# Segment sums of a graph network by pairs of 500 edges and 128 nodes, instead of by steps of 128-edge tiles

## The reference

```python
def _L1_gnn_ref(x, src, dst, ...):            # once
    m = jax.nn.relu(x[src])
    agg = jax.ops.segment_sum(m, dst, num_segments=N)
    h = (1.0 + eps[0]) * x + agg
...
def _L2_gnn_ref(node_feat, ...):              # 4 times
    trans = jnp.einsum('nd,tod->tno', h, W_edge) + b_edge[:, None, :]
    msg = trans[etypes, src]
    a = jax.ops.segment_sum(msg, dst, num_segments=N)
    h = _gru_cell(a, h, W_ih, W_hh, b_ih, b_hh)
```

## Time and profile before

| | |
|---|---|
| median of 3 runs | 12611.91 us |
| lowest and highest of them | 12582.9 and 12612.57 us |
| span of the profiled execution | 12521.9 us |
| outside the span, to the median and to the lowest run | 90.0 and 61.0 us |
| share of the span: PE, DVE, POOL, ACT | 53%, 44%, 50%, 19% |
| clock granted to TensorE, mean | 0.701 |

### The profile page before, as it was taken

The page is one execution under the profiler, slowest core; times in us unless marked ns, Lnnn a source line. Parts: engine busy times, 40 slices in busy tenths (PEclk is TensorE's granted clock), DMA queues, the critical chain, the costliest instruction groups (busy, mean ns, idle before and its releaser), DMA issues. The chain is left out here.

```text
span 12521.9 us, 164892 instructions
## 1 busy us (share of the span) xinstructions
PE 6604.1 (53%) x35059; PEld 5552.8 (44%) x35060; DVE 5536.9 (44%) x13969; ACT 2372.4 (19%) x5039; POOL 6320.5 (50%) x6362
## 2 busy tenths in 40 slices
PE   4555686555686555785335333433533353355555
PEld 3555674555665555663223222333322332234444
DVE  4444664444664444753334233433433343345555
ACT  1222452222452222452000000000000000011111
POOL 2555432556422555423663666366366636635663
PEclk7777898777897777896556555655655565567777
DMA  2333321334322333321111111111111111112221
GB/s 81 113 113 113 99 80 55 116 114 118 101 69 64 114 115 114 102 63 29 44 44 55 46 42 43 56 44 43 47 53 44 43 57 43 43 25 87 82 80 58
DMA packets 697724, 893.26 MB, mean 71 GB/s; under 512 B 148412, under 2 KB 442581, under 8 KB 697500
## 3 DMA queue, kind: packets, MB, share of 16 engines
q0 software_dynamic: 198368, 429.61, 13.4%
q1 hardware_dynamic: 497412, 461.38, 11.8%
q10 hardware_dynamic: 1848, 1.12, 0.0%
HBM read 698.40 MB, written 193.14 MB: 71 GB/s over the span
## 5 line engine op out<-in xcount | busy, mean ns | idle before, releaser
L761 POOL DMA_INDIRECT l_sums_ring<-table_typed,index x2512 | 2436.2, 970 | 1951.2 <-ACT index L862 1181.2
L897 PE MATMUL psum<-l_sums_ring,select 128*128 x6720 | 1630.0, 419 | 3214.3 <-DVE select L793 2600.8
L761 POOL DMA_INDIRECT acc<-table_x,index x2016 | 2039.8, 1012 | 2141.2 <-DVE index L756 1556.4
L897 PEld LDWEIGHTS psum<-l_sums_ring,select 128*128 128x128 f32 x6720 | 1404.0, 309 | 3443.1 <-issue 3443.1
L823 DVE TENSOR_TENSOR acc<-acc,psum 128x128 f32 (+1 forms) x4032 | 1160.8, 288 | 3336.4 <-remote 2288.8
L793 DVE TENSOR_TENSOR select<-iota_row,dst_local 128x512 f32<-128x512 f32 (+1 forms) x1680 | 1070.8, 638 | 340.0 <-issue 318.8
L1015 PE MATMUL psum<-ident,select 128*128 128x128 f32 x2016 | 437.8, 356 | 1465.0 <-DVE acc L974 593.5
L990 DVE TENSOR_TENSOR l_scores_prod<-l_scores_key,psum 128x512 f32<-128x512 f32 x504 | 345.7, 686 | 1777.3 <-ACT l_scores_key L963 1303.7
L862 ACT COPY index<-tile_idx 128x4 int32 (+1 forms) x785 | 150.3, 193 | 4510.2 <-remote 2770.2
L1015 PEld LDWEIGHTS psum<-ident,select 128*128 128x128 f32 x2016 | 300.3, 181 | 1540.3 <-issue 827.3
L761 POOL DMA_INDIRECT l_pass_ring<-table_kv,index x672 | 674.7, 1004 | 598.5 <-issue 242.4
(11 more groups left out here) (319 smaller groups left out, 10103.9 us busy)
## 6 DMA issues: line engine op xcount, KB each, us to landing
acc<-in_edge_attr_dram SPq DMA_DIRECT2D x2016, 64.0 KB
rows_dram<-l_scores_mixT SPq DMA_DIRECT2D x504, 256.0 KB
l_values_ring<-rows_dram SPq DMA_DIRECT2D x504, 256.0 KB
table_typed<-l_rows_rows SPq DMA_DIRECT2D x40, 1024.0 KB, 4.2
l_sums_ring<-table_typed,index POOLq DMA_INDIRECT x2512
acc<-table_x,index POOLq DMA_INDIRECT x2016
l_pass_ring<-table_kv,index POOLq DMA_INDIRECT x672
table_x<-l_rows_rows SPq DMA_DIRECT2D x40, 256.0 KB, 2.2
```

The costliest lines, as they stand in the source:

```text
L761: pool.indirect_dma_start(out=ring[:, at, u, :], out_offset=None, in_=table, in_offset=bass.IndirectOffsetOnAxis(ap=index[:, at % REGIONS, ...
L897: ins = pe.matmul(sums(r, u), select[:, r, u, :], rows, start=True, stop=True)
```

## The change

The edges are cut into 640 tiles of 125 instead of 625 of 128, so that four tiles, a region, are 500 edges and there are exactly 160 regions. The list of the pass is no longer of tiles and blocks but of pairs (region, block): 160 + 40 = 200. For a pair, one select is made over all four tiles of the region against one block, the four products accumulate in one PSUM slice, and one addition goes into `acc`. A region that reaches into a second block is walked again with that block. Register values are read for four pairs at a time.

```diff
-TILE_REGIONS = -(-TILES // GROUP)
+EDGES = 125
+SUM_TILES = E // EDGES
+TILE_REGIONS = SUM_TILES // GROUP
...
-                pool.indirect_dma_start(out=ring[:, at, u, :], out_offset=None, in_=table,
-                                        in_offset=bass.IndirectOffsetOnAxis(ap=index[:, at % REGIONS, u:u + 1], axis=0)
+                pool.indirect_dma_start(out=ring[0:n, at, u, :], out_offset=None, in_=table,
+                                        in_offset=bass.IndirectOffsetOnAxis(ap=index[0:n, at % REGIONS, u:u + 1], axis=0)
...
+                        def pick(s, k, column):
+                            at_least(dve, p_summed, s - (REGIONS - 1))
+                            dve.scalar_tensor_tensor(
+                                out=select[:, k, :, :], in0=dst_all[:, bass.ds(column, GROUP)].unsqueeze(2).broadcast_to([P, GROUP, P]),
+                                scalar=pair_start[:, bass.ds(s, 1)], in1=iota_row[:].unsqueeze(1).broadcast_to([P, GROUP, P]),
+                                op0=ALU.subtract, op1=ALU.is_equal).then_inc(p_selected, 1)
+
+                        def body(i):
+                            last = isinstance(i, int) and i == PAIR_TURNS - 1
+                            entries = by_step(dve, pick_row, (i * REGIONS + 1) * 2, 2 * REGIONS, TILE_REGIONS * GROUP)
+                            for k in range(REGIONS):
+                                s = i * REGIONS + k
+                                to_block, column = entries[2 * k], entries[2 * k + 1]
+                                if not (last and k == REGIONS - 1):
+                                    pick(s + 1, (k + 1) % REGIONS, column.with_bounds(min_val=0, max_val=(TILE_REGIONS - 1) * GROUP))
+                                dve.wait_ge(p_summed, s + 1)
+                                at_least(dve, p_added, s)
+                                to = acc[:, bass.ds(to_block.with_bounds(min_val=0, max_val=BLOCKS) * ACC_W, D)]
+                                dve.tensor_tensor(to, to, sums(k), ALU.add).then_inc(p_added, 1)
-                        make_select(dve, 0, 0)
-
-                        def body(i):
-                            for r in range(REGIONS):
-                                if nxt := led(i, r, 1):
-                                    at_least(dve, p_summed, region_of(*nxt) - (REGIONS - 1))
-                                    make_select(dve, *nxt)
-                                add_blocks(dve, sums, i, r, D, blocks_of(dve, i, r))
-                        turns(dve, body)
...
                     @b.tensor
                     def _(pe):
                         def body(i):
-                            for r in range(REGIONS):
-                                j = region_of(i, r)
-                                needs, *at = by_step(pe, plan_row, j * PLAN, PLAN, TILE_RING * GROUP * D)
-                                pe.wait_ge(p_selected, j + 1)
+                            entries = by_step(pe, sum_row, i * (2 * REGIONS), 2 * REGIONS, TILE_RING * GROUP * D)
+                            for k in range(REGIONS):
+                                s = i * REGIONS + k
+                                needs, at = entries[2 * k], entries[2 * k + 1]
+                                pe.wait_ge(p_selected, s + 1)
                                 pe.wait_ge(p_landed, needs.with_bounds(min_val=1, max_val=TILE_REGIONS))
-                                at_least(pe, p_added, (j - (REGIONS - 1)) * GROUP)
+                                at_least(pe, p_added, s - (REGIONS - 1))
+                                at = at.with_bounds(min_val=0, max_val=(TILE_RING - 1) * GROUP * D)
                                 for u in range(GROUP):
-                                    rows = slots[:, bass.ds(at[u].with_bounds(min_val=0, max_val=(TILE_RING * GROUP - 1) * D), D)]
-                                    ins = pe.matmul(sums(r, u), select[:, r, u, :], rows, start=True, stop=True)
+                                    rows = slots[0:EDGES, bass.ds(at + u * D, D)]
+                                    ins = pe.matmul(sums(k), select[0:EDGES, k, u, :], rows, start=u == 0, stop=u == GROUP - 1)
                                 ins.then_inc(p_summed, 1)
```

More of the change, by code:

```diff
@@ new lines, in _ @@
+                    link(dve.tensor_copy(dst_tf, dst_ti[:]))
+                    dve.sem_inc(s_pair, 1)
+                    dve.wait_ge(s_pair_pe, 1)
+                    for c in range(PAIR_C):
+                        link(dve.tensor_scalar(behind, psum[0:PAIR_K, 4, 0:TILE_REGIONS], pair_no[:, c:c + 1], None, ALU.is_lt))
+                        link(dve.tensor_reduce(pair_at[:, 0, c:c + 1], behind, AX_X, ALU.add))
+                    link(dve.tensor_scalar(pair_at[:, 0, :], pair_at[:, 0, :], float(TILE_REGIONS - 1), None, ALU.min))
@@ L456, in _ @@
                             at = (c % n_bank) * n_row
-                            ins = pe.transpose(psum[:, bank + c // n_bank, at:at + n_row], of[:, c, :], ident[0:n_row, 0:n_row])
+                            wide = P if n_row == ROW_K else EDGES
+                            ins = pe.transpose(psum[0:wide, bank + c // n_bank, at:at + n_row], of[:, c, :], ident[0:n_row, 0:n_row])
                         ins.then_inc(s_pe, 1)
+                    pe.wait_ge(s_pair, 3)
+                    for c in range(TILE_COLS):
+                        at = (c % n_bank) * TILE_ROWS
+                        pe.transpose(psum[0:EDGES, 2 + c // n_bank, at:at + TILE_ROWS], dst_tf[:, c, :], ident[0:TILE_ROWS, 0:TILE_ROWS])
+                    pe.matmul(psum[0:PAIR_K, 4, 0:TILE_REGIONS], ones[0:1, 0:PAIR_K], region_reach[:], start=True, stop=True).then_inc(s_pair_pe, 1)
+                    pe.wait_ge(s_pair, 4)
+                    for c in range(2 * PAIR_C):
+                        ins = pe.transpose(psum[0:1, 5, c * PAIR_K:(c + 1) * PAIR_K], pair_at[:].rearrange("k a c -> k (a c)")[:, c:c + 1],
+                                           ident[0:PAIR_K, 0:PAIR_K])
+                    ins.then_inc(s_pair_pe, 1)
+                    pe.wait_ge(s_pair, 5)
+                    pe.matmul(psum[:, 6, 0:PAIRS], ones[0:1, :], pair_row[:, 1, :], start=True, stop=True).then_inc(s_pair_pe, 1)
         def at_least(eng, sem, value):
@@ L782, in pair @@
                 for k in range(at, at + n):
-                    gather(pool, ring, table, k)
+                    gather(pool, ring, table, k, EDGES)
             with pool.Fori(0, TILE_TURNS) as i:
@@ L910, in gat_score_pass @@
                 key = sb(f"{name}_key", [P, 2, GROUP, D], F32, tmp)
-                prod = sb(f"{name}_prod", [P, GROUP, D], F32, tmp)
+                prod = acc[:, 2 * RING:2 * RING + GROUP * D].rearrange("p (u f) -> p u f", f=D)
                 part = sb(f"{name}_part", [P, GROUP, GAT_HEADS], F32, tmp)
@@ L1044, in gat_value_pass @@
                 msg = sb(f"{name}_msg", [P, REGIONS, GROUP, W], F32, tmp)
-                away = sb(f"{name}_away", [P, 2, GROUP, P], F32, tmp)
+                away = w3[:].rearrange("p (a u) f -> p a u f", a=2)
                 def values(r):
```

139 lines of the change are left out of this document (98 added, 41 removed).

## The result

The changed kernel took 12692.15 us (median of 4 runs, 12674.36 to 12710.38), the kernel before 12612.24 us beside it (4 runs, 12582.9 to 12630.22): a ratio of 1.0067 with a 95% interval of 1.0054 to 1.0079, so 0.67% or 80 us slower. The forecast was 12,770, slower, for reasons that turned out to hold only in part.

A forecast was written before the change was run, and what follows sets the result against it. The prediction took the sum passes as gather streams stopped by PE's late reports; 5 x (15 + 24 - 9) + 10 = +160 us gave a span of about 12,682, plus 90 us, so 12,770, range 12,200 to 13,000.

The forecast's parts named there:

- gathers and gaps between them: First sum pass: 640 gathers of 125 rows at an unchanged 1.25 us instead of 628, +15 us a pass.
- stops: Waits of POOL on a full ring: 35.7 instead of 30 a pass, +24 us, bounds -129 and +54 us.
- rest: Forecast -9 us a pass: credit for DVE's issue gaps, which fall by 83 us while DVE mostly waits for PE.
- the bound of 0.06: Upper bound on POOL's extra time for a gather of 125 rows: +0.06 us a gather, +38 us a pass.
- The sentence by the rule of the Trainium skill: Transfers: 125 rows use 5 DMA engines instead of 16, 0.8 us instead of 0.25, +0.55 us a pass.
- The sign named for this case: In the changed profile: fewer than 27 stops a pass would mean late reports came from DVE or all engines' issue.
- Times five: First-pass terms multiplied over five sum passes: 5 x (15 + 24 - 9) + 10 = +160 us.
- DVE: Sum passes: additions and selects fall from 309 to 196 us a pass, the new select taking 692 ns.
- Table stage: Small DVE operations, PE round trips and loads added once ahead of the passes: +10 us.
- The 90 us outside the span: Median of runs 12611.9 lies 90 us above the span 12521.9, so about 12,682 of span became 12,770.
- DVE is the bound: Rival, sum passes: fewer DVE instructions let pairs keep up with gathers; 12,050, half-way 12,330; chance 0.34, wholly or in part.
- the gather of 125 rows costs POOL more: Rival: +0.06 us on 3200 gathers, +192 us on top of the sum, 12,960; chance 0.05.

## Why the prediction was right in its sign, and where it failed

The first pass by its terms, forecast and measured:

| | before | forecast of the change | measured change |
|---|---|---|---|
| gathers and gaps between them | 805.0 | +15 | 968.6, +163.6 |
| stops | 129.3 | +24 | 0, -129.3 |
| rest | 18.7 | -9 | 7.4, -11.3 |
| pass | 953 | +30 | 976, +23 |

- **Gathers.** The step "if a gather costs POOL the same ... I take 0" failed. It costs 0.24 us more, four times the bound of 0.06 that I took from the rows of 96 and 128. Both counts are multiples of 16, so these rows could not bound the cost of a count that isn't. The sentence by the rule of the Trainium skill said how many engines 125 rows use and stopped at the transfer. From the start of the first region's fourth gather to PE's first product it takes 5861.37 - 5857.63 = 3.74 us, against 2.79 before: +0.95, of which 0.25 are POOL's longer gather, so 0.70 where the estimate by the rule had 0.55. That comes once a pass. What costs the time is POOL's part, 640 times. (The 785 us of the prediction for the gathers of before were measured as 805, so half of its 39 us "for start and tail" were gathers.) These are the rows, changed kernel, then the one before:

```profile
5857.63 1.20 POOL L827 DMA_INDIRECT l_sums_ring<-table_x,index  x1 [0.30 <-issue]
...
5861.37 2.07 PE L983 MATMUL psum<-l_sums_ring,select 125*128 x8 [19.75 <-SPq L919]
```

```profile
5811.54 0.95 POOL L761 DMA_INDIRECT l_sums_ring<-table_x,index  x1 [0.31 <-issue]
...
5814.33 2.07 PE L897 MATMUL psum<-l_sums_ring,select 128*128 x8 [17.53 <-SPq L848]
```

- **Stops.** "What limits them during gathers is PE's lateness, and PE's work a step is the same" was right for gathers of 128 rows: pairs with them had passes of 979 (990 forecast) and 25 stops (35.7 forecast). But the lateness was taken as given, with its cause unnamed, and it went with the row count. The sign named for this case ("if there are fewer than 27 stops a pass, the reports were late because of DVE or of the sum of issues") points to the wrong cause: the steps with 125 rows keep all of DVE's additions and have no stops. The two errors nearly cancel, 163.6 - 129.3 = 34 against 15 + 24 = 39. That the forecast came within 80 us is luck in this sense: a mechanism that it didn't have, the dearer gather, paid for stops that it kept.
- **Times five.** The change was forecast as +160 us and measured as +80. The terms are those of the first pass, which was the shortest of the five before (952.6 us, on average 961) and is not in the changed kernel (976.6, on average 976.4). Its +24 us times five would be 120; the five passes together gave 77.
- **DVE.** Its busy time fell to 199 us a pass (196 forecast). The new select takes 748 ns, not 692. Little of it shows in the pass, as forecast: pairs with 128 rows are not faster than steps with 128 rows (979 against 961, and 0.53% slower in all on one chip).
- **Table stage.** About 4 us instead of 10.
- **The 90 us outside the span.** This reading was wrong. Each run now lists its own time and span, 1.8 us apart (12674.36 and 12672.5). The profiled execution of before, 12521.9, was simply some 60 us faster than the fastest of the four listed runs (12582.9). With 2 us instead of 90 my sum gives 12,684 for that execution and 12,772 for the median of 12,612 plus 160, so the forecast stands, for another reason.
- **Rivals.** The stops vanished, as in "DVE is the bound", but not because of DVE; and "the gather of 125 rows costs POOL more" came true at four times its price. The two together weren't priced, and together they are the measured kernel.

What stays open: by which path indirect gathers of 128 rows slow register instructions and reports of other engines, why gathers of 125 rows don't, and why the mix of 127, 126, 124 and 96 rows doesn't either. It is also open why every full kernel with 128 rows comes, over its five passes, to 1.50 to 1.55 us of the pass for each gather, with and without stops (1.62 with the products made twice). A kernel with tiles of 120 or 126 edges wasn't tried.

## What to carry to other kernels

Before the height of gathered tiles is changed for the sake of a round number of tiles, look at its largest divisor up to 16: here 125 rows cost POOL 1.21 us where 126 cost 0.98 and 128 cost 0.97. A wait that names no engine is a cause still to be found: the run with plain transfers in place of the gathers (961 us a pass down to 410) showed at once that these 550 us hang on the gathers and not on PE or DVE. When two engines seem late for no reason, compare the register instructions of an idle third: SP's 53 ns against 530 was the clearest sign in all traces.

## What was not expected of the hardware

- POOL's time for an indirect gather of 512-byte rows: 920 to 1013 ns for 96, 112, 120, 126 and 128 rows, 1226 for 125, 1301 for 124, 2605 for 127.
- The queue's packets rose from 200288 to 353888 from pairs with 128 rows to pairs with 125: 153600 / 3200 = 48 more for each gather of fewer rows. In the first pass a gather of 125 rows makes 15 of 4096 bytes, 5 of 512, 33 of 32 and 27 of 4; one of 128 rows makes 16 of 4096 and 16 of 4.
- Back-to-back gathers of 128 rows stretch SP's 53 ns instruction to 530 on average and 1395 at most. In the kernels with 128 rows PE's update comes up to 12.9 to 20.6 us after the last product, against 0.015 us with 125 rows (0.47 with the products made twice). Plain transfers at more than twice the rate do neither.
- Less work on PE made the pass slower: 1000 us with half the products, 961 with all, 1016 with double.
